# Constant-tile matmuls in TensorE's pauses, and skip and output projection moved behind the last sums, in a four-block convolution and scan kernel

## The chip, the cores and the metric

The kernel runs on one core of a Trainium2 chip. The metric is the device time of one execution in microseconds (us); every comparison is of medians. "PE" is TensorE, "DVE" VectorE, "ACT" ScalarE, "POOL" GpSimd, "SP" the engine that issues most DMAs.

## What is computed

The input is `x`, 8 images of 32 x 32 pixels with 64 channels, float32. Four blocks follow one another, each added to its input after a group normalisation over 32 groups:

```python
x = x + _L0_conv_ref(_gn(x), ...)   # two depthwise 3x3 convolutions, Sobel, 5 diffusion steps
x = x + _L1_conv_ref(_gn(x), ...)   # dense 3x3 convolution, 64 to 64 channels
x = x + _L2_conv_ref(_gn(x), ...)   # layer norm, Mamba block, skip, layer norm, projection
x = x + _L3_conv_ref(_gn(x))        # orthonormal 2-D DCT of each image
```

In the third block a selective scan runs over 1024 positions, for 128 inner channels and 16 states; its output is gated with silu(z), multiplied by the output projection, the scaled normalised input is added (the skip), and after another layer norm the last projection follows:

```python
y = selective_scan(xs, delta, A, Bm, Cm, D) * silu(z)
y = y @ out_proj_w.T + skip_scale * x_norm
y = layer_norm(y, ln_g, ln_b) @ proj_w.T + proj_b
```

## The kernel before, in words

Two images lie side by side on the 128 partitions (64 channels each); such a pair is called `k`, and two pairs make a half `h`. The program treats half 0 and half 1 one after the other. Each engine has its program written out by hand in the order in which it is to run; semaphores join them. `SCANS = 64` scan steps belong to a half: 4 images (`j`) times 16 states.

**The stage in front of the scan** (PE lines 677 to 700). PE ends the dense convolution of pair 1 (`conv_part(1, 1)`, L444), turns the normalised pixels into channels (`xn_channels`, eight 128 x 128 transposes by L433), runs a tiny group mean (L438), the input projection (`in_proj`, L513 for x and L519 for z), the transposes of `n2_pixels(h, 1)` (L433 again), and `x_proj` (L450). DVE follows with `causal` (L1454, then three of L1457) and then the second pair's layer norm; ACT computes silu and the copies (nearly every ACT instruction is recorded at L789).

**The scan** (PE lines 711 to 773). For step s ACT makes the decay, PE brings the row of B into PSUM (`b_rows`, L534, with the constant bf16 tile `sel` of 96 partitions as its weights) or transposes an input scaled by ACT (`turn_scaled`, L433); DVE multiplies where needed (L1493) and scans (L1498); POOL multiplies the states with the row of C (L332) into one of two buffers `HC`, so product s waits for `sum_of(s - 2)`; PE adds the product to PSUM tile `PS[3]` (`sum_of`, L564, four matmuls of 512 columns). The rows of C come by DMA from DRAM, queued by SP. PE calls `fill(s + 2)` and then `sum_of(s - 1)` in loop step s. After 16 steps DVE gates the sum of one image (`gate`, L1502).

At loop step 60 PE also runs `skip(1)` (L572, 16 short matmuls) and `out_proj(h, 2)` (L578, 16 matmuls of 64 columns), between `sum_of(59)` and `fill(63)`; `out_proj(h, 3)` comes after the last sum and needs the last gate.

**Between the halves** DVE goes from the last scan of half 0 to the Sobel sums of half 1 (`sobel_sums`, L224 and L225, then L1338), to the gate (L1502), three more Sobel operations (L1342, L1343, L1345) and the mean of the layer norm (`center`, L1305).

**The last stage** (PE lines 775 to 783) treats pair 1 of half 1 alone: `out_proj(3)`; `center` on DVE (L1305, L1312) with a small ACT step between; a square on ACT; a reduction on DVE (L1317); the variance on ACT, which raises the semaphore `lvar`; the root on POOL (L315); `normalize` on DVE (L1325); `xn2_channels` on PE (L433); a scaling on ACT; `last_proj` (L450); `add_block` on DVE (L1506); `x3_pixels` (L433) and the group statistics; `first_dct` (L600), `keep_x3` (L613), `scale` on ACT, `a2_pixels` (L433), a copy, `second_dct` (L618), two copies and the stores. `center` raises the semaphore `xc`.

Of the kernel before, what the change touches and what calls it, by code (L numbers as in the profile page):

```python
# [15 lines left out]
P = 128  # L16
BLK = L // P
HB = 16
BANK = 512
# [23 lines left out]
def fused_blocks(nc, x, vec, mats, conv_w, in_w, xbc_w, xdt_w, dtp_w, out_w, proj_w, out):  # L43
# [9 lines left out]
    with ctx:  # L53
# [5 lines left out]
        def S(name):  # L59
            if name not in sems:  # L60
                sems[name] = ctx.enter_context(nc.semaphore("s_" + name))
            return sems[name]
# [19 lines left out]
        sel = ctx.enter_context(nc.sbuf_tensor("sel", [96, D_STATE * P], bf16))  # L82

        def mt(name):
            return mat[:, M[name] * P:(M[name] + 1) * P]
# [6 lines left out]
        PS = [ctx.enter_context(nc.psum_tensor(f"ps{i}", [P, 2 * BANK], fp32)) for i in range(4)]  # L92
# [50 lines left out]
        def img(t):  # L143
            return t[:, 0:L].rearrange("p (h w) -> p h w", h=H)
# [7 lines left out]
        def blk(t, k):  # L152
            return t[:, k * P:(k + 1) * P]

        def half(t, n):
            return t[:, n * BANK:(n + 1) * BANK]
# [265 lines left out]
        def _(pe):  # L422
            mm = nc.tensor.matmul
# [16 lines left out]
            def conv_taps(ps, taps, frame, n, chosen, first=0):  # L440

                for tap in chosen:
                    dy, dx = tap // 3, tap % 3
                    last = mm(half(ps, n), taps(tap), frame[:, dy + HB * n:dy + HB * n + HB, dx:dx + W],  # L444
                              start=(tap == first), stop=(tap == 8))
                return last
# [13 lines left out]
            def depthwise(h, k, w, n):  # L460
# [9 lines left out]
                if n == 1:  # L470
                    last.then_inc(S(f"a_conv{w}"), 1)

            def divergence(h, k):
                a = A[k]
                pe.wait_ge(S(f"a{k}_gg1"), 2 * h + 2)
                g, ps = img(a["g"]), img(PS[2 * k])
                for n in range(2):
                    r = slice(HB * n, HB * n + HB)
                    mm(ps[:, r, :], mt("roll_diff"), img(a["g1"])[:, r, :], start=True, stop=False)
                    mm(ps[:, r, 0:31], ident, g[:, r, 1:32], start=False, stop=False)  # L480
                    mm(ps[:, r, 31:32], ident, g[:, r, 0:1], start=False, stop=False)
                    mm(ps[:, r, 1:32], mt("neg_ident"), g[:, r, 0:31], start=False, stop=False)
                    last = mm(ps[:, r, 0:1], mt("neg_ident"), g[:, r, 31:32], start=False, stop=True)
                last.then_inc(S("a_div"), 1)
# [11 lines left out]
            def conv_part(k, n, chosen):  # L496
                return conv_taps(PS[2 * k], lambda tap: blk(convw, tap), frm(D[k]["cfz"]), n, chosen)

            def n2_pixels(h, k):
                pe.wait_ge(S("n2"), 2 * h + k + 1)  # L500
                transposes(D[k]["N2"], PS[2 * k]).then_inc(S("n2T"), 1)
# [20 lines left out]
            def x_proj(h, k, b):  # L522
                i = 2 * h + b
                xs = D[k]["XS"][:, b * L:b * L + L]
                pe.wait_ge(S(f"xs{k}"), i + 1)
                project(PS[2 * k], dtw[:, :], xs).then_inc(S(f"dt{k}"), 1)
                pe.wait_ge(S(f"sz{k}"), i + 1)
                project(PS[2 * k + 1], xbcw[:, :], xs).then_inc(S(f"bc{k}"), 1)
# [28 lines left out]
            def sum_of(h, s):  # L557
                j, first = s // D_STATE, s % D_STATE == 0
                if first:
                    pe.wait_ge(S("y_read"), ONE + 4 * h + j)  # L560
                    plain(pe)
                pe.wait_ge(S("hc"), SCANS * h + s + 1)
                for n in range(2):
                    last = mm(half(PS[3], n), ident, half(HC[s % 2], n), start=first, stop=True, skip_group_check=True)  # L564
                last.then_inc(S("sum"), 1)
                if first:
                    for n in range(2):
                        mm(half(PS[3], n), diagD[:, :], half(two_images(j, "XS"), n), start=False, stop=True, skip_group_check=True)

            def skip(k):  # L570
                for n in range(BLK):
                    mm(blk(PS[2], n), blk(D[k]["XNC"], n), skipI[:, :], start=(n % 4 == 0), stop=False, skip_group_check=True)  # L572

            def out_proj(h, j):
                k, b = j // 2, j % 2
                pe.wait_ge(S("y_read"), ONE + 4 * h + j + 1)
                for n in range(BLK):
                    last = mm(blk(PS[2], n)[:, C * b:C * b + C], blk(D[k]["SZ"], BLK * b + n), outw[:, :],  # L578
                              start=False, stop=True, skip_group_check=True)
                if b == 1:  # L580
                    last.then_inc(S("mo"), 1)

            def xn2_channels(h, k):
                pe.wait_ge(S("xn2"), 2 * h + k + 1)
                transposes(F[k]["XN"], final_ps(h, k)).then_inc(S("xn2T"), 1)
# [39 lines left out]
            for h in range(HALVES):  # L625
# [58 lines left out]
                conv_part(1, 0, range(5, 9))  # L684
                n2_pixels(h, 0)
                conv_part(1, 1, range(9)).then_inc(S("c_conv"), 1)

                xn_channels(h, 0)
                group_mean(D[1], h, 2, 1)
                in_proj(h, 0, 0)  # L690
                n2_pixels(h, 1)
                x_proj(h, 0, 0)
                in_proj(h, 0, 1)
                xn_channels(h, 1)
# [16 lines left out]
                for s in range(1, SCANS):  # L711
                    if s == 2 * D_STATE - 2:
                        pe.wait_ge(S("bcs1"), ONE + 4 * h + 4)
                        plain(pe)
                    fill(h, s + 2)
                    sum_of(h, s - 1)
                    if s == 2:
                        pe.wait_ge(S("rx1"), 2 * h + 2)
                        turn_du(h, 0)
                    if s == 3:  # L720
                        turn_rows(h)
                    if s == 5:
                        pe.wait_ge(S("kept"), 5 * h + ROWS_TURNED)
                        turn_du(h, 1)
                    if s == 23:
                        if h + 1 < HALVES:
                            pe.wait_ge(S("group1"), g_var(h + 1, 0))
                        else:
                            pe.wait_ge(S("kept"), turned(h, 1))
                        turn_du(h, 2)  # L730
                    if s == 28:
                        pe.wait_ge(S("kept"), turned(h, 2))
                        turn_du(h, 3)
                    if s == 32:
                        pe.wait_ge(S("kept"), turned(h, 3))
                        skip(0)
                    if h + 1 < HALVES:
                        if s == 7:
                            pe.wait_ge(S("kept"), turned(h, 1))
                            x_channels(h + 1, 0, PS[2])  # L740
                        if s == 12:
                            group_mean(A[0], h + 1, 0, 0)
                        if s == 15:
                            pe.wait_ge(S("a_x"), 2 * h + 3)
                            pe.wait_ge(S("group0"), g_var(h + 1, 0))
                            x_channels(h + 1, 1, PS[2])
                        if s == 20:
                            group_mean(A[1], h + 1, 0, 1)
                    if s == 33:
                        out_proj(h, 0)  # L750
                    if s == 34:
                        out_proj(h, 1)
                    if s == 41:
                        xn2_channels(h, 0)
                    if s == 44:
                        last_proj(h, 0)
                    if s == 48:
                        group_mean(D[0], h, 3, 0)
                    if s == 50:
                        x3_pixels(h, 0)  # L760
                    if s == 52:
                        first_dct(h, 0)
                    if s == 54:
                        a2_pixels(h, 0)
                    if s == 57:
                        keep_x3(h, 0)
                        second_dct(h, 0)
                    if s == 60:
                        pe.wait_ge(S("ot"), 2 * h + 1)
                        skip(1)  # L770
                        out_proj(h, 2)
                sum_of(h, SCANS - 1)
                out_proj(h, 3)

            h = HALVES - 1
            xn2_channels(h, 1)
            last_proj(h, 1)
            x3_pixels(h, 1)
# [941 lines left out]
```

## Time and profile before

| | |
|---|---|
| runs | 1035.80, 1036.42, 1038.41 us; median 1036.42 |
| the profiled execution | 1035.26 us, its span on the core 1033.2 us |
| mean granted TensorE clock | 0.926 of full speed |
| busy share | PE 82%, DVE 82%, POOL 57%, ACT 55% |
| chain that ended last | PE 42%, DVE 38%, ACT 7%, issue 6%, POOL 6% |
| DMA | 72 GB/s over the span |

The chain says which engine the end waited for at each moment. Granted clock 1.00 is 2.4 GHz and 0.50 is 1.2 GHz; the profile has no other level, and a value between is a stretch that holds both. In the timeline, the bracket behind a row is the idle time in front of it on its engine and what ended it.

### The profile page before, as it was taken

To read this page: it belongs to the slowest core of one execution; us is meant where nothing else is said; L and a number is where in the kernel's file an instruction comes from. 1 tells how busy PE (TensorE), PEld (TensorE's weight loads), DVE (VectorE), ACT (ScalarE), POOL (GpSimd) and SP (SyncE) were. 2 spreads that over 40 slices of the span, in tenths; PEclk is the share of its full clock that TensorE was granted. 3 is DMA by queue.
4 is the path that set the end of the run, shared out by engine and by line. 5 is a ranking of instruction groups with operands and counts; after the bars stand their busy time and mean duration, and the time that the engine had idled before them with its cause. 6 is when DMAs were issued, how large, how long until landed. Compare 5 with 4: busy or idle time off the path is not lost.

```text
span 1033.2 us, 8216 instructions
## 1 busy us (share of the span) xinstructions
PE 843.9 (82%) x2690; PEld 421.4 (41%) x2690; DVE 848.9 (82%) x657; ACT 569.7 (55%) x953; POOL 590.7 (57%) x262
## 2 busy tenths in 40 slices
PE   3986998977288898899889599897738889889955
PEld 2432443433144445446445244343314334545633
DVE  5999887268999898998997978636899999899841
ACT  3733332146748886688575332303684878668802
POOL 2444996020668686877354789501065979677730
PEclk8996999989689999999999899998967999999977
DMA  3000000002344454445100100000113545444411
GB/s 100 1 0 0 0 0 1 0 0 56 79 129 163 139 186 144 144 161 143 44 0 1 20 0 0 0 1 0 56 46 102 176 151 183 143 143 162 146 39 20
DMA packets 33206, 74.35 MB, mean 72 GB/s; under 512 B 15753, under 2 KB 15889, under 8 KB 33169
## 3 DMA queue, kind: packets, MB, share of 16 engines
q1 hardware_dynamic: 31760, 72.58, 21.7%
q0 software_dynamic: 320, 1.05, 0.4%
q8 instruction: 19, 0.31, 0.1%
q10 hardware_dynamic: 1088, 0.26, 0.1%
q14 instruction: 19, 0.15, 0.0%
HBM read 70.73 MB, written 3.15 MB: 72 GB/s over the span
## 4 chain that ended last, share of the span: by engine, by line
PE 42%; DVE 38%; ACT 7%; issue 6%; POOL 6%; DMA 0%; DVEq 0%; SPq 0%; POOLq 0%; ACTq 0%
DVE arena L1498 11%; PE ps L672 9%; PE ps L444 9%; PE ps L564 8%; ACT arena L789 5%; DVE ps L1493 4%; PE ps L433 3%; PE ps L666 3%; POOL arena L332 3%; DVE arena L1457 3%; PE ps L450 2%; DVE arena L1355 2%; POOL dr L315 1%; PE ps L534 1%; DVE arena L1487 1%
## 5 line engine op out<-in xcount | busy, mean ns | idle before, releaser
L332 POOL TENSOR_TENSOR arena<-arena 128x1024 f32<-128x1024 f32 x128 | 304.2, 2383 | 113.9 <-DVE arena L1498 60.7
L1498 DVE TENSOR_TENSOR_SCAN arena<-arena,ps 128x1024 f32<-128x1024 f32 x128 | 289.6, 2281 | 18.0 <-POOL arena L332 8.2
L564 PE MATMUL ps<-arena,mat 128*128 128x512 f32 x512 | 251.7, 616 | 8.8 <-POOL arena L332 7.9
L789 ACT ACTIVATE arena<-arena 128x128 f32<-128x128 f32 (+4 forms) x346 | 146.4, 493 | 106.2 <-DVE arena L1425 75.7
L789 ACT ACTIVATE arena<-arena,Amat 128x1024 f32<-128x1024 f32 x128 | 146.1, 1144 | 88.7 <-DVE arena L1498 85.1
L564 PEld LDWEIGHTS ps<-arena,mat 128*128 128x128 f32 x512 | 95.7, 197 | 90.8 <-issue 68.5
L672 PE MATMUL ps<-arena,mat 128*128 128x512 f32 x240 | 106.3, 592 | 0.0
L1493 DVE TENSOR_TENSOR ps<-arena,ps 128x1024 f32<-128x1024 f32 x72 | 87.2, 1210 | 7.7 <-PE ps L534 5.7
L789 ACT ACTIVATE arena<-ps 128x1024 f32<-128x1024 f32 (+2 forms) x58 | 53.7, 934 | 67.3 <-PE ps L433 22.0
L444 PE MATMUL ps<-arena,diag 128*128 128x512 f32 x192 | 86.6, 609 | 2.1 <-ACT arena L789 2.1
L534 PE MATMUL ps<-arena,sel 96*128 96x512 bf16 x144 | 45.5, 401 | 49.5 <-DVE arena L1498 49.5
L433 PE MATMUL ps<-mat,arena 128*128 128x128 f32 x448 | 61.0, 282 | 26.2 <-DVE arena L1325 14.7
L433 PEld LDWEIGHTS ps<-mat,arena 128*128 128x128 f32 x448 | 52.8, 146 | 53.0 <-issue 29.0
L444 PE MATMUL ps<-arena,convw 128*128 128x512 f32 x144 | 66.9, 621 | 7.2 <-ACT arena L789 7.2
L672 PEld LDWEIGHTS ps<-arena,mat 128*128 128x128 f32 x240 | 45.6, 190 | 57.4 <-issue 57.4
L789 ACT ACTIVATE ROWS<-arena 128x128 f32<-128x128 f32 x224 | 68.2, 389 | 0.0
L444 PEld LDWEIGHTS ps<-arena,diag 128*128 128x128 f32 x192 | 37.0, 195 | 47.6 <-issue 45.4
L321 POOL TENSOR_TENSOR arena<-arena 128x1024 f32<-128x1024 f32 x8 | 21.6, 2704 | 60.0 <-DVE arena L1482 60.0
L315 POOL TENSOR_TENSOR dr<-dv,cpow 128x16 f32<-128x16 f32 x8 | 24.0, 3006 | 55.8 <-DVE dv L1320 43.3
L311 POOL TENSOR_TENSOR dgn<-dgn,cpow 128x1 f32<-128x1 f32 x12 | 7.3, 608 | 85.1 <-DVE dgn L1279 82.5
L348 POOL TENSOR_TENSOR arena<-arena 128x1024 f32<-128x1024 f32 x8 | 25.9, 3242 | 46.4 <-DVE arena L1380 33.0
L534 PEld LDWEIGHTS ps<-arena,sel 96*128 96x128 bf16 x144 | 11.3, 100 | 91.7 <-DVE arena L1498 73.6
(169 smaller groups left out, 1351.2 us busy)
## 6 DMA issues: line engine op xcount, KB each, us to landing
arena<-bc_rows SPq DMA_DIRECT2D x128, 512.0 KB, 3.8
out<-arena SPq DMA_DIRECT2D x28, 64.0 KB, 2.2
xres<-x POOLq DMA_DIRECT2D x4, 256.0 KB, 5.1
bc_rows<-ROWS SPq DMA_DIRECT2D x8, 128.0 KB, 1.9
xres<-x SPq DMA_DIRECT2D x4, 256.0 KB, 4.3
convw<-conv_w SPq DMA_DIRECT2D x1, 576.0 KB
mat<-mats SPq DMA_DIRECT2D x1, 448.0 KB, 3.5
inw<-in_w SPq DMA_DIRECT2D x1, 256.0 KB
```

What stands on the lines that cost most here:

```text
L315: tt(t["r"][:, :], t["v"][:, :], cpow[:, :], ALU.pow).then_inc(S("lrstd"), 1)
L332: tt(HC[s % 2], HS[s % 2], CB[s % 4], ALU.mult).then_inc(S("hc"), 1)
L433: last = nc.tensor.transpose(blk(dst, n), blk(src, n), ident)
L444: last = mm(half(ps, n), taps(tap), frame[:, dy + HB * n:dy + HB * n + HB, dx:dx + W], start=(tap == first), stop=(tap == 8))
L534: last = mm(half(PS[s % 2], n), blk(sel, s % D_STATE), half(two_images(s // D_STATE, "BCS"), n)[0:96, :], start=True, stop=True)
L564: last = mm(half(PS[3], n), ident, half(HC[s % 2], n), start=first, stop=True, skip_group_check=True)
L666: last = mm(half(mix, n), ident, half(a["g"], n), start=False, stop=False, skip_group_check=True)
L672: last = mm(half(mix, n), mt(mname), half(a[src], n), start=False, stop=(name == "e"), skip_group_check=True)
L789: return nc.scalar.activation(out_, in_, func, bias=bias, scale=scale, accum_out=accum_out)
L1457: stt(d["XI"][:, t:L], PS[2 * k][:, 0:L - t], w[3 - t], d["XI"][:, t:L], ALU.mult, ALU.add)\
L1493: tt(PS[q][:, :], two_images(j, "DU"), PS[q][:, :], ALU.mult).then_inc(S("dbu"), 1)
L1498: nc.vector.tensor_tensor_scan(HS[q], DA[q], PS[q][:, :], 0.0, ALU.mult, ALU.add).then_inc(S("scan"), 1)
```

## The change

A new helper `spin(ps, n)` multiplies the first 128 columns of `sel` as weights with 512 columns of `sel`, n times, into the second bank of a PSUM tile, which nobody reads before it is overwritten. It is called at two places in the stage in front of the scan (in both halves) and at three in the last stage, twice behind an added wait. `skip(1)` and `out_proj(h, 2)` leave loop step 60: the first now stands in front of `sum_of(63)`, the second behind it, in both halves.

```diff
+            def spin(ps, n):
+                for _ in range(n):
+                    mm(half(ps, 1), sel[:, 0:P], sel[:, 0:BANK], start=True, stop=True, skip_group_check=True)
...
                 conv_part(1, 1, range(9)).then_inc(S("c_conv"), 1)
+                spin(PS[1], 8)

                 xn_channels(h, 0)
                 group_mean(D[1], h, 2, 1)
                 in_proj(h, 0, 0)
                 n2_pixels(h, 1)
+                spin(PS[3], 14)
                 x_proj(h, 0, 0)
...
-                    if s == 60:
-                        pe.wait_ge(S("ot"), 2 * h + 1)
-                        skip(1)
-                        out_proj(h, 2)
+                pe.wait_ge(S("ot"), 2 * h + 1)
+                skip(1)
                 sum_of(h, SCANS - 1)
+                out_proj(h, 2)
                 out_proj(h, 3)

             h = HALVES - 1
+            spin(PS[0], 10)
+            pe.wait_ge(S("xc"), 4 * h + 4)
+            spin(PS[0], 6)
+            pe.wait_ge(S("lvar"), 4 * h + 4)
+            spin(PS[0], 13)
             xn2_channels(h, 1)
```

## Rows read from the trace of the kernel before

**Rows 1.** The page: granted TensorE clock in tenths, 40 slices of the span.
```profile
PEclk8996999989689999999999899998967999999977
```
**Rows 2.** Windows: us, busy of PE, PEld, DVE, ACT, POOL, then PEclk, DMA share, GB/s.
```profile
211.30:213.60 2.30, 0.00 (x0) 0.00 (x0) 2.30 (x3) 0.00 (x0) 0.42 (x1) 1.00 0.00 0
215.10:221.70 6.60, 6.19 (x9) 3.00 (x10) 2.65 (x7) 3.47 (x3) 0.55 (x1) 0.50 0.00 0
223.50:226.30 2.80, 0.00 (x0) 0.00 (x0) 2.75 (x3) 1.27 (x2) 0.00 (x0) 1.00 0.00 0
...
219.90:262.60 42.70, 27.72 (x72) 11.61 (x71) 38.20 (x35) 27.25 (x27) 3.40 (x2) 0.98 0.12 34
```
**Rows 3.** Timeline, PE, in front of half 0's scan.
```profile
216.10 3.78 PE L513 MATMUL ps<-arena,inw 128*128 128x512 f32 x4
...
226.39 1.98 PE L450 MATMUL ps<-arena,dtw 128*128 128x512 f32 x4 [2.92 <-ACT arena L789]
```
**Rows 4.** Timeline, PE, the input projection in half 1.
```profile
708.19 3.78 PE L513 MATMUL ps<-arena,inw 128*128 128x512 f32 x4 [0.26 <-ACT arena L789]
```
**Rows 5.** Chain: the tile `sel` as weights, at full and at half clock.
```profile
973.42 0.43 PE ps L534 x2
...
785.83 1.03 PE ps L534 x2
```
**Rows 6.** Timeline, last scan steps of half 1.
```profile
980.00 1.08 SPq L259 DMA_DIRECT2D arena<-bc_rows  x2
980.15 1.95 PE L572 MATMUL ps<-skipI,arena 128*128 128x128 f32 x16
...
984.75 2.29 DVE L1498 TENSOR_TENSOR_SCAN arena<-arena,ps 128x1024 f32<-128x1024 f32 x1 [0.79 <-PE ps L433]
...
986.61 4.64 POOL L332 TENSOR_TENSOR arena<-arena 128x1024 f32<-128x1024 f32 x2 [3.60 <-PE ps L564]
...
993.33 1.22 DVE L1502 TENSOR_TENSOR arena<-ps,arena 128x1024 f32<-128x1024 f32 x1 [6.29 <-PE ps L564]
...
994.61 2.00 PE L578 MATMUL ps<-outw,arena 128*128 128x64 f32 x16 [1.32 <-DVE arena L1502]
```
**Rows 7.** Windows, columns as in rows 2: just behind the last C rows.
```profile
985.20:986.40 1.20, 1.20 (x4) 0.51 (x3) 1.20 (x1) 0.00 (x0) 0.00 (x0) 1.00 0.01 3
```
**Rows 8.** Timeline, POOL and DVE, from half 0's last scan to half 1.
```profile
496.51 5.70 POOL L332 TENSOR_TENSOR arena<-arena 128x1024 f32<-128x1024 f32 x2 [3.60 <-PE ps L564]
496.86 3.15 DVE L224 TENSOR_TENSOR arena<-arena 128x1088 f32<-128x1088 f32 x1
...
499.94 3.42 DVE L225 TENSOR_TENSOR arena<-arena 128x1088 f32<-128x1088 f32 x1
```
**Rows 9.** Timeline, DVE, the first of these operations in half 0, POOL idle.
```profile
24.70 1.29 DVE L224 TENSOR_TENSOR arena<-arena 128x1088 f32<-128x1088 f32 x1 [3.72 <-ACT arena L789]
```
**Rows 10.** Windows of the last stage, columns as in rows 2.
```profile
993.30:996.50 3.20, 1.90 (x16) 1.86 (x16) 1.22 (x1) 0.00 (x0) 0.00 (x0) 1.00 0.00 0
996.70:1006.20 9.50, 0.00 (x0) 0.00 (x0) 4.78 (x4) 1.55 (x3) 2.90 (x1) 0.50 0.00 0
...
1013.70:1017.00 3.30, 1.09 (x8) 0.86 (x8) 3.20 (x5) 0.47 (x1) 0.00 (x0) 1.00 0.00 0
```
**Rows 11.** Timeline of the last stage.
```profile
998.15 1.23 DVE L1312 TENSOR_TENSOR ps<-ps,dm 128x1024 f32<-128x1024 f32 x1 [0.28 <-ACT dm L789]
...
1002.11 2.90 POOL L315 TENSOR_TENSOR dr<-dv,cpow 128x16 f32<-128x16 f32 x1 [10.86 <-ACT dv L789]
...
1006.32 1.97 PE L433 MATMUL ps<-mat,arena 128*128 128x128 f32 x8 [9.72 <-DVE arena L1325]
...
1009.59 3.78 PE L450 MATMUL ps<-arena,projw 128*128 128x512 f32 x4 [1.30 <-ACT arena L789]
...
1017.67 3.37 PE L600 MATMUL ps<-mat,arena 128*128 128x128 f32 x16
...
1020.88 1.95 PE L613 MATMUL ps<-mat,arena 128*128 128x128 f32 x16
```

## Prediction

> **What bounds the kernel now.** I read the page first: PE and DVE share the chain (42% and 38%), and the granted clock is full nearly everywhere but in a few slices [rows 1]. Three places matter for this change, so I cut them out with windows and timelines.
>
> In front of the scan PE ends the convolution near 211.2, pauses 2.5 us, runs eight transposes, and from 215.1 to 221.7 the clock is 0.50 [rows 2]. The input projection takes 3.78 us there, where four matmuls of the same shape take 1.98 us at full clock a little later [rows 3]; half 1 shows 3.78 us again [rows 4]. DVE waits for that projection and is then busy for 38.2 of 42.7 us up to the scan [rows 2], so what PE loses, the scan's start loses. A pause alone does not lower the clock: PE was idle from 223.5 to 226.3 at 1.00 [rows 2].
>
> At the end of each half PE runs skip (1.95 us with its latency) and out_proj(2) (as long as out_proj(3), 2.00 us; 3.5 us for both, back to back) in front of the transposes and sums that the last scan and the last products wait for: DVE idles 0.79 us before the last scan and POOL 3.60 us before its last two products [rows 6], half 0 the same [rows 8].
>
> In the last stage everything is one chain. The clock is 0.50 from 996.7 on, while PE has nothing to do, and back at 1.00 in the window from 1013.7 [rows 10]. Three PE steps of the chain run at the lower clock [rows 11]: the transposes (1.97 us, against 1.09 in that later window), the projection (3.78), and, after one more fall, the first DCT (3.37 us for 16 matmuls, where the 16 of L613 take 1.95 right behind).
>
> **The change, part by part.** *Price of a spin.* Two `sel` matmuls of 512 columns take 0.43 us, so one is 0.215 us; the pair costs 1.03 us at half clock with its latency, so some 0.43 us each [rows 5]. 8, 14, 10, 6 and 13 of them are 1.7, 3.0, 2.1, 1.3 and 2.8 us at full clock.
>
> *Spins in front of the scan.* Eight fill 211.0 to 212.8; the transposes come at 213.7, so they cost nothing; if that cover were gone they cost up to 1.7 us. If the clock then holds, the projection ends 1.8 us earlier (3.78 - 1.98) [rows 3]. ACT's silu is not in the way, since DVE's four causal operations (5.2 us) lie between. Today PE waits 2.92 us before `x_proj` [rows 3]. Both the wait's start and its end move forward (by 2.3 and 1.8 us, since L519 is faster too), so fourteen spins run from 221 until 224 and `x_proj` becomes ready at 226.4 - 1.8 = 224.6. They cost nothing too. Bounds of the gain: 0 (clock falls as before) to 1.8 per half. I take 1.8, since the pause of 2.8 us with a full clock [rows 2] shows that some work around a pause is enough, and the spins put work where there was none: 3.6 us for two halves.
>
> *Skip and out_proj(2) out of loop step 60.* The transposes for step 63 no longer stand behind 3.5 us of PE work, so the last scan starts when the one before it ends: 984.0, not 984.75. Sum 60 ends near 983.4, so product 62 starts at 984.0, not 986.6, and product 63 ends at 984.0 + 4.64 = 988.7, not 991.3 [rows 6]. The last two C rows are queued at 980.0, and the DMA engines are idle from 985.2 on [rows 6, 7], so both are there before product 63 begins (986.3). The first of them is needed at 984.0; no row shows its landing, and I count it as just in time. Then PE: sum 62 until 988.1, skip 1.78 until 989.9, sum 63 until 991.6, result at 991.9 where it was 993.3. Here skip stands in front of the last sum and takes back 1.2 us of the 2.6. out_proj(2) runs until 993.4 beside the gate (1.22 us, until 993.15), and out_proj(3) takes its 2.0 us behind both: 995.3, not 996.6 [rows 6]. Gain in half 1: 1.3 us. Bounds: -2.0 (the products don't move: skip costs 1.78 less PE's short wait there, and out_proj(2) outlasts the gate by 0.5) to 1.5. The added wait for `ot` holds nothing up: SP's stores waited for the same copy and are issued before the C rows at 980.0 [rows 6]. SP's, ACT's and POOL's queues are not changed.
>
> *The same at the end of half 0.* Here DVE doesn't wait for the gate but goes on with the Sobel sums, and these collide with POOL: 3.15 and 3.42 us beside POOL's products [rows 8], 1.29 us alone [rows 9]. That is 4.0 us for two products. With product 62 moved beside the scan (which POOL does not slow: 2.29 us, and 4.64 us for two products [rows 6]) only one product collides: DVE would go 496.2, + 1.2 + 1.2 + one product of 2.35, so 501.0 where it was 503.4. Gain 2.3 us (0.8 from the scan, 1.55 from the collision). Sum 63 is ready at 501.9 and the gate comes at 502.2. Bounds: 0.8 (both still collide) to 2.8.
> Each of the two DVE operations is longer by about one POOL product (1.9 and 2.1 us against 2.3), so one product less beside them is about 1.55 to 2 us less.
>
> *Spins in the last stage.* All of DVE's and ACT's steps come 1.3 us earlier: `xc` at 999.4 - 1.3 = 998.1, `lvar` at 1002.1 - 1.3 = 1000.8, `xn2_channels` ready at 1006.3 - 1.3 = 1005.0 [rows 11]. Ten spins follow out_proj(3) until 997.2, six run until 999.4, thirteen until 1003.6. Behind each added wait nothing is queued but the spins and `xn2_channels`, which waits for later work anyway; cover left is 1.4 us. If the clock holds until the projection, transposes save 1.97 - 1.09 = 0.9 and projection 3.78 - 1.98 = 1.8 [rows 3, 10, 11]. No spin stands between the projection and the first DCT; there PE has 1.09 us of work in over 4 us, and that is the window behind which the clock fell before [rows 10]. I therefore leave the first DCT at 3.37 us; if it held, 1.4 us more, as L613's 1.95 us for 16 such matmuls shows [rows 11]. Term: 2.7, bounds 0 to 4.1.
>
> *Sum:* 3.6 + 1.3 + 2.3 + 2.7 = 9.9 us from the profiled execution's 1035.26 us (span 1033.2, 2.1 us around it unchanged): 1025.4. The median of the runs stands 1.2 us above that execution, which would make 1026.5. I take 1025.8, between the two, since one execution doesn't tell which of them is the odd one.
>
> **The rivals.** *Part of the clock gain is lost, and not the same part in each run.* The clock fell behind the pause at 211.3, but not behind the one at 223.5 [rows 2], so where it falls doesn't follow from the pause alone, and eight transposes between two waits stay bare in each spun stretch. One half lost is 1025.8 + 1.8 = 1027.6, the tail lost 1028.5. For it too: the fall at 996.6 came with 1.9 us of PE work in the 3.2 us before [rows 10].
> The Trainium skill (TensorE: Matmul & The Clock Gate, "What's actually happening") says that the activity monitor is free-running and not tied to the kernel's start, so that a change of clock lands at another matmul from run to run. By that rule the median over runs loses one or two microseconds of the clock's 6.3, and runs of the changed kernel differ by that much; no run here shows it yet.
>
> *The spins don't hold the clock at all* (bf16, 96 of 128 rows, no result used: perhaps they don't count). Then only the order pays: 1035.3 - 3.6 = 1031.7, 1032.8 against the median. For it: no row shows such matmuls alone at full clock. Against: in the scan, where they alternate with the sums, the page reads 9 in nearly every slice [rows 1].
>
> *The order gives nothing* (product 62 still waits for its C row, or skip in front of sum 63 takes back all): clock alone, 9.9 - 3.6 = 6.3: 1028.9 to 1030. For it: the DMA engines are still at work until 985 [rows 7].
>
> *Slower than before:* the spins themselves run at half clock and delay the work behind them. Place: the fourteen in front of `x_proj`. At 0.43 us each they take 6.0 us; from 223.4 they end at 229.4 where `x_proj` ran at 226.4: 3.0 us lost in each half [rows 3], and thirteen from 1002.1 end at 1007.7 where the transposes ran at 1006.3, 1.4 us late [rows 11]. With the order's 3.6 us back: 6.0 + 1.4 - 3.6 = 3.8, so 1039.1. It decides where the clock is still 0.50 when the fourteen start; before, it was back at 1.00 behind 221.7, before that point, and PE's 6.2 busy microseconds brought it there [rows 2].
>
> *The change does nothing:* spins not holding the clock and products not moving together: 1035 to 1036.
>
> **How the numbers follow.** Forecast, 1023.3 (first DCT and the order's upper bounds too) to 1027.4: 0.44. Part of the clock gain lost, 1027.4 to 1029: 0.20. Order gives nothing, 1028.9 to 1030.5: 0.12. Spins don't hold, 1031.5 to 1032.8: 0.14. Nothing: 0.06. Slower: 0.04. Range 1022.8 to 1031.8: it takes in the first three cases, and of the fourth its near edge. About 0.3% (3.1 us) is what a measurement of this kernel can tell from no change; all but the last two cases lie beyond it (below 1033.3): faster 0.90, same 0.06, slower 0.04.
>
> **What the profile would show.** The stretch from the convolution's end to `x_proj` at 1.00 in both halves, the first L513 at 1.98 us and DVE's work behind it 1.8 us earlier, counted from the convolution's end; the last scan following the one before without 0.79 us; POOL's last products starting at that scan's start; L224 or L225 at 1.3 us at the half's boundary; L433 at 1.09 and L450 at 1.98 us in the last stage, L600 still 3.37. The forecast is wrong if a window with spins reads 0.50, if PE's idle time before `x_proj` or `xn2_channels` is gone (spins in the way), or if POOL's product 62 waits for a DMA.

## The result, and the profile after

The changed kernel takes 1026.99 us (median of 4 runs, 1025.57 to 1029.02); the kernel before takes 1036.11 us (4 runs, 1035.52 to 1038.41). The ratio is 0.990, 95% interval 0.9884 to 0.9917: faster by 1.0%. The forecast was 1025.8 us, between 1022.8 and 1031.8. The profiled execution took 1025.8 us with a span of 1023.6 us; before it was 1035.26 and 1033.2, so 9.5 us are to be accounted for. The mean granted clock rose from 0.926 to 0.953.

The timeline of the changed kernel in front of half 0's scan (start, length, engine, line; 12 lines of code more shift DVE's and ACT's line numbers, and PE's from L477 on by 6, so L513 is now L519):

```profile
209.78 1.89 PE L477 MATMUL ps<-sel 96*128 96x512 bf16 x8
...
214.84 1.98 PE L519 MATMUL ps<-arena,inw 128*128 128x512 f32 x4 [0.31 <-ACT arena L801]
...
216.86 1.28 DVE L1466 TENSOR_SCALAR arena<-ps,vecs 128x1024 f32<-128x1024 f32 x1 [0.88 <-PE ps L519]
...
219.25 3.19 PE L477 MATMUL ps<-sel 96*128 96x512 bf16 x14
...
223.33 1.98 PE L450 MATMUL ps<-arena,dtw 128*128 128x512 f32 x4 [0.90 <-ACT arena L801]
```

The projection takes 1.98 us where it took 3.78 [rows 3], and both trains of spins end before the work behind them is ready: PE still idles 0.90 us in front of `x_proj` (2.92 before [rows 3]).

The end of half 0 and the start of half 1, where the rows before are [rows 8]:

```profile
488.27 4.47 DVE L1510 TENSOR_TENSOR_SCAN arena<-arena,ps 128x1024 f32<-128x1024 f32 x2
...
491.29 5.71 POOL L332 TENSOR_TENSOR arena<-arena 128x1024 f32<-128x1024 f32 x2 [1.67 <-DMA arena<-bc_rows]
...
492.65 2.13 DVE L224 TENSOR_TENSOR arena<-arena 128x1088 f32<-128x1088 f32 x1
...
494.70 3.44 DVE L225 TENSOR_TENSOR arena<-arena 128x1088 f32<-128x1088 f32 x1
```

The last two scans follow each other without a gap. But POOL's idle time of 1.67 us in front of product 62 now ends with a DMA, the row of C. The first of the two scans, whose states the product needs, ended at 490.6 (488.27 + 2.29), so the row costs the last 0.7 us of that wait, and a part of product 62 still collides with L224 (2.13 us, 3.15 before).

The end of half 1 and the last stage, against [rows 6, 11]:

```profile
972.65 1.08 SPq L259 DMA_DIRECT2D arena<-bc_rows  x2
...
974.33 4.47 DVE L1510 TENSOR_TENSOR_SCAN arena<-arena,ps 128x1024 f32<-128x1024 f32 x2
...
977.25 4.65 POOL L332 TENSOR_TENSOR arena<-arena 128x1024 f32<-128x1024 f32 x2 [1.58 <-DMA arena<-bc_rows]
...
981.47 1.95 PE L578 MATMUL ps<-skipI,arena 128*128 128x128 f32 x16
983.25 1.88 PE L570 MATMUL ps<-arena,mat 128*128 128x512 f32 x4
984.97 3.68 PE L584 MATMUL ps<-outw,arena 128*128 128x64 f32 x32
985.17 1.22 DVE L1514 TENSOR_TENSOR arena<-ps,arena 128x1024 f32<-128x1024 f32 x1 [6.37 <-PE ps L570]
...
998.37 1.09 PE L433 MATMUL ps<-mat,arena 128*128 128x128 f32 x8 [1.26 <-DVE arena L1337]
...
1000.76 1.98 PE L450 MATMUL ps<-arena,projw 128*128 128x512 f32 x4 [1.29 <-ACT arena L801]
...
1004.78 1.81 PE L433 MATMUL ps<-mat,arena 128*128 128x128 f32 x8 [2.04 <-DVE arena L1518]
...
1007.71 3.78 PE L606 MATMUL ps<-mat,arena 128*128 128x128 f32 x16 [0.52 <-ACT arena L801]
```

Here too the first of the two scans ends at 976.6 and the product starts at 977.25, 4.6 us after SP issued the row; the page of the kernel before has a median of 3.8 us from issue to landing for these loads.

The same in windows of the changed kernel (columns as in rows 2):

```profile
988.50:1004.70 16.20, 9.84 (x43) 4.09 (x42) 6.82 (x5) 2.75 (x4) 2.90 (x1) 1.00 0.00 1
1005.00:1011.50 6.50, 5.98 (x28) 5.49 (x27) 2.16 (x8) 1.02 (x1) 0.56 (x1) 0.50 0.00 0
```

Transposes (1.09 us) and projection (1.98) run at the full clock, as far as the spins reach. Then the clock falls at 1005, and now the transposes of `x3_pixels` (1.81 us, 1.09 before) and the first DCT (3.78 us, 3.37 before) run at 0.50. That the spins bring this about isn't shown: kernels without a spin in the last stage show it too (below, the order alone).

**Where the 9.5 us come from.** Each row goes from the end of the row above to the point that it names, in one timeline; the gain is before minus after:

| stretch | before | after | gain |
|---|---|---|---|
| start to the end of half 0's convolution (first L1441, now L1453) | 211.25 | 209.98 | 1.3 |
| to DVE's first causal step, half 0 | 8.67 | 6.88 | 1.8 |
| to the end of half 0's last scan | 277.0 | 275.9 | 1.1 |
| to the end of half 1's convolution | 206.2 | 205.2 | 1.0 |
| to DVE's first causal step, half 1 | 8.82 | 6.88 | 1.9 |
| to the end of half 1's last scan | 275.0 | 274.0 | 1.0 |
| to the last gate | 6.29 | 6.37 | -0.1 |
| to `add_block` | 20.08 | 17.61 | 2.5 |
| to the last copy | 14.06 | 15.17 | -1.1 |

The first row lies in front of everything that the change touches. All fourteen profiles of this case share the code up to there, and in them that point lies between 209.98 and 211.80 us.

### The profile page after: what moved, and what is told of

Read it like the earlier page. It is cut to its first block, busy times and chain, and to the rows that moved or that the text cites. A ratio compares the mean times of both kernels' runs of the same rounds, so it can differ in the third digit from the quotient of the medians.

```text
span 1023.6 us, 8362 instructions
## 1 busy us (share of the span) xinstructions
PE 845.6 (83%) x2763; PEld 423.3 (41%) x2763; DVE 847.7 (83%) x657; ACT 569.6 (56%) x953; POOL 590.9 (58%) x262
## 3 DMA queue, kind: packets, MB, share of 16 engines
HBM read 70.73 MB, written 3.15 MB: 72 GB/s over the span
## 4 chain that ended last, share of the span: by engine, by line
DVE 39%; PE 39%; ACT 7%; POOL 6%; issue 6%; DMA 1%; SPq 1%; DVEq 0%; POOLq 0%; ACTq 0%
DVE arena L1510 12%; PE ps L678 10%; PE ps L444 9%; PE ps L570 6%; ACT arena L801 6%; DVE ps L1505 4%; POOL arena L332 3%; PE ps L672 3%; DVE arena L1469 3%; PE ps L433 3%; DVE arena L1367 2%; PE ps L450 2%; POOL dr L315 1%; DVE arena L1499 1%; DVE arena L1466 1%
```

## The experiments

Eleven variants ran, and the changed kernel once more. The kernel before had medians of 1037.55, 1036.71 and 1037.62 us in the three groups in which they were measured, so ratios are the better measure; a difference between two variants in microseconds is of their medians, and where the ratios say something else, it is told. The theory: spins hold the clock and pay only through the PE steps behind them; the new order pays by the last scan of each half and by the collision of POOL and DVE; the two don't depend on each other. The rivals: one of the two does nothing; or the falls of the clock are accidents of single executions.

**The order alone.**

```diff
-                spin(PS[1], 8)
-                spin(PS[3], 14)
-            spin(PS[0], 10)
-            pe.wait_ge(S("xc"), 4 * h + 4)
-            spin(PS[0], 6)
-            pe.wait_ge(S("lvar"), 4 * h + 4)
-            spin(PS[0], 13)
```

> The change without its five spins and their waits; skip and out_proj(2) stand where the change puts them. Theory (both parts pay, independently): the last scan of each half starts 0.79 us earlier, the boundary between the halves gives 1.0 us more, the last stage gives 0.3 back: 2.3 us below the kernel before; the clock is 0.50 in front of both scans and behind the last gate, as before. Rival (the order alone gives nothing, its gain in the changed kernel was the clock's): within 0.5 us of before.

Measured: 1034.88 us, ratio 0.9977 (0.9964 to 0.9989), 2.4 us (1.1 to 3.7). Its windows show the half clock back in all three places, the last one without the recovery that the kernel before had at 1013.7:

```profile
213.50:220.20 6.70, 5.99 (x10) 2.67 (x9) 2.63 (x8) 3.73 (x3) 0.55 (x1) 0.50 0.00 0
705.10:711.70 6.60, 5.89 (x9) 2.68 (x9) 2.54 (x8) 3.73 (x3) 0.55 (x1) 0.50 0.00 0
995.20:1018.90 23.70, 10.88 (x35) 7.54 (x36) 8.38 (x13) 3.77 (x5) 3.46 (x2) 0.50 0.00 0
```

The order pays as expected, and without any spin. Two more readings of this kernel, in PE's timeline of the last stage:

```profile
1013.09 1.97 PE L433 MATMUL ps<-mat,arena 128*128 128x128 f32 x8 [2.04 <-DVE arena L1511]
...
1016.17 3.38 PE L606 MATMUL ps<-mat,arena 128*128 128x128 f32 x16 [0.68 <-ACT arena L794]
```

The transposes of `x3_pixels` run at half clock here as in the changed kernel, and the first DCT takes as long as before or longer (3.78 us in the kernel with only the front spins), with no spin in the stage. From `add_block` to the last copy it is 14.90 us, and 15.31 and 14.78 in the other two kernels below that have no spin in this stage; the kernel before, at 14.06, is the lowest of the four.

**The spins alone**, with skip and out_proj(2) back in loop step 60.

```diff
+                    if s == 60:
+                        pe.wait_ge(S("ot"), 2 * h + 1)
+                        skip(1)
+                        out_proj(h, 2)
                 sum_of(h, SCANS - 1)
-                out_proj(h, 2)
                 out_proj(h, 3)
```

> The five spins with skip and out_proj(2) back in loop step 60. Theory: 1.8 and 1.9 us in front of the two scans, 2.7 us in the last stage, less up to 1.0 us where the first DCT runs wholly at half clock: 5.4 to 6.4 us below before. Rival (without the new order out_proj(3) alone stands before the ten spins, the clock has fallen there already, and they run at 0.50): only the 3.7 us of the front stages, and the ten spins take 4.3 us.

Measured: 1033.91 us, ratio 0.9961 (0.9946 to 0.9976), 4.0 us: less than the theory's 5.4. The nine runs fall into two groups, four from 1031.26 to 1031.76 and five from 1033.91 to 1034.78. The profile is of the second group, and shows three losses. The boundary of the halves, from half 0's last scan to half 1's convolution, took 207.70 us, 206.24 before. In half 0 the clock fell in spite of the eight spins (8.4 us to the first causal step, 6.9 in half 1). And in the last stage:

```profile
1001.09 5.73 PE L477 MATMUL ps<-sel 96*128 96x512 bf16 x13 [1.18 <-ACT dv L802]
1006.61 1.60 PE L433 MATMUL ps<-mat,arena 128*128 128x128 f32 x8
```

```profile
996.50:1000.80 4.30, 2.73 (x12) 0.90 (x10) 2.82 (x3) 1.32 (x3) 0.00 (x0) 1.00 0.00 0
1000.90:1007.60 6.70, 6.51 (x18) 3.03 (x19) 1.23 (x1) 0.13 (x1) 2.90 (x1) 0.50 0.00 0
```

The clock fell in the pause of 1.18 us behind the six spins, the thirteen took 5.73 us instead of 2.98, and the transposes started with no idle time in front of them, 1.3 us after DVE's `normalize` (1004.04 + 1.23) had made them ready. That is the mechanism of my slow rival, in one place and for 1.3 us. The ten spins took 2.32 us, so they did not start at half clock, as the rival had it. The first group of runs would be the executions without some of these losses; their mean granted clock is 0.947 to 0.948 against 0.936 to 0.942 in the second, which fits, but they have no profile.

**Only the spins in front of the scan** (the edit above, and):

```diff
-            spin(PS[0], 10)
...
-            spin(PS[0], 13)
```

> Only the eight and the fourteen spins in front of the scan, in both halves. Theory: 3.7 us below before, the first L513-type projection at 1.98 us in both halves. Rival (the fall moves elsewhere): the projection is fast but the clock falls somewhere later before the scan, and less than 2 us are left.

Measured: 1033.76 us, ratio 0.9971 (0.9960 to 0.9982), 3.0 us. Both halves show 6.88 us to the first causal step, so the 3.7 us are there in the stage; in the boundary of the halves 1.5 us went the other way (207.75 us from scan end to convolution's end, 206.24 before, with one more stretch at 0.50 at 524 to 527). The spins alone gave hardly more than the spins in front of the scan: by the ratios, the last stage's were worth 1 us with the old order, by the medians nothing (1033.91 and 1033.76 us), and the intervals overlap.

**The whole change without the spins of the last stage.**

```diff
                 out_proj(h, 3)

             h = HALVES - 1
-            spin(PS[0], 10)
...
-            spin(PS[0], 13)
             xn2_channels(h, 1)
```

> The whole change without the spins and waits of the last stage. Theory (the spins there give 2.7 us with the new order, less 1.0 us at the first DCT): 1.5 to 2.5 us above the changed kernel (1027.0 to 1027.3); xn2's transposes 1.97 and the last projection 3.78 us. Rival (behind the new order out_proj(2) and out_proj(3) alone keep the clock up): within 0.5 us of the changed kernel.

Measured: 1029.54 us, ratio 0.9927 (0.9912 to 0.9942), against 0.9900 and 0.9906 for the change itself: they are worth 2.2 to 2.8 us. Gate to `add_block` is 20.13 us again, 17.6 in the changed kernel. This stretch shows the effect of the spins most steadily: 20.08 to 20.28 us in the four profiled kernels without spins there, 17.61 or 17.62 in nine of the ten profiles with them, and 19.20 in the kernel with spins alone. This profile shows a front stage that was lost with the spins in it, as the one with spins alone:

```profile
216.60:219.80 3.20, 3.15 (x4) 1.51 (x5) 0.51 (x3) 1.95 (x3) 0.55 (x1) 0.50 0.00 0
```

**The changed kernel again**, with no edit.

> The changed kernel again, unaltered, as the neighbour of the next three and for the spread of its executions. Theory (the clock's falls lie at points that are not tied to the program, and the spun stretches are too thin to be safe in each run): executions spread over 3 to 5 us, in steps of about 1.5 to 2 us, and this profile shows the clock falling at other points than the first one. Rival (the program sets the falls): the same falls as in the first profile, spread under 1 us.

Measured: 1027.25 us (6 runs, 1026.31 to 1028.79), ratio 0.9906 (0.9891 to 0.9921). With the first measurement ten executions lie between 1025.57 and 1029.02, 3.5 us; the steps that I had expected in them don't stand out. The same program, the same stretch of the diffusion steps, first and second profile:

```profile
80.00:86.70 6.70, 3.78 (x4) 1.17 (x4) 6.70 (x7) 1.24 (x1) 0.17 (x1) 0.50 0.00 0
87.00:90.00 3.00, 0.20 (x1) 0.24 (x2) 2.93 (x4) 1.45 (x2) 2.74 (x2) 1.00 0.00 0
```

```profile
79.00:95.40 16.40, 9.30 (x11) 3.62 (x12) 16.34 (x13) 7.61 (x11) 8.51 (x3) 0.50 0.00 0
```

Near the same work the clock was at 1.00 in one execution and at 0.50 in the other, and half 0's convolution ended at 209.98 and at 211.4. So some falls move from run to run, and the 1.3 us in the first row of the table are not the change's. Most falls do not move: between the two scans the clock is at 0.50 from 581.7 to 592.0 us in the first profile and from 583.7 to 594.0 in the second, where the same work comes 1.6 to 1.9 us later, and the stretch behind `add_block` starts 2.2 and 2.3 us behind that step. So of the theory and the rival each has a part.

**More spins in front of the scan** (11 for 8, 4 behind `xn_channels`, 17 for 14).

```diff
-                spin(PS[1], 8)
+                spin(PS[1], 11)
                 xn_channels(h, 0)
+                spin(PS[3], 4)
...
-                spin(PS[3], 14)
+                spin(PS[3], 17)
```

> The whole change with more spins in front of the scan: 11 for 8, 4 new ones behind xn_channels, 17 for 14, sized so that they end before the work behind them is ready. Theory (thin stretches let the clock fall in some runs): both front stages take 6.9 us from the convolution's end to DVE's first causal operation in every profile; the median is 0.5 to 1.5 us below the changed kernel's, with less spread. Rival (the eight were enough, or spins have no such effect): no difference.

Measured: 1026.57 us (5 runs, 1026.10 to 1027.25), ratio 0.9900 (0.9884 to 0.9915). The median is 0.7 us under its neighbour's and the spread 1.2 us against 2.5, as expected but inside the intervals. The profiles say more. Ten profiles here, the changed kernel's two among them, have the eight spins; in their twenty stages the clock fell in three, all of them in half 0 (8.4 to 8.5 us to the first causal step instead of 6.9). The two kernels with the dense spins show 6.9 in four of four. Four of four is no proof at a loss of three in twenty.

**More spins in the last stage.**

```diff
-            spin(PS[0], 10)
+            spin(PS[0], 13)
...
-            spin(PS[0], 6)
+            spin(PS[0], 11)
...
-            spin(PS[0], 13)
+            spin(PS[0], 18)
             xn2_channels(h, 1)
+            spin(PS[1], 6)
             last_proj(h, 1)
+            spin(PS[1], 9)
             x3_pixels(h, 1)
+            spin(PS[1], 3)
             group_mean(D[1], h, 3, 1)
+            spin(PS[1], 3)
             first_dct(h, 1)
```

> The whole change with more spins in the last stage: 13, 11 and 18 for 10, 6 and 13, and 6, 9, 3 and 3 new ones behind the second transposes, the last projection, x3_pixels and the group mean. Theory: the clock stays at 1.00 from the last gate to the second DCT; transposes 1.09, first DCT 1.95 instead of 3.4 to 3.8 us: 2.5 us below the changed kernel. Rival (the new spins delay the steps they stand before): PE's idle time before L433 or L600 is zero and the gain is under 1 us or a loss.

Measured: 1023.98 us (5 runs), ratio 0.9881 (0.9865 to 0.9898), 3.3 us below its neighbour (2.6 by the ratios).

```profile
988.78 9.71 PE L477 MATMUL ps<-sel 96*128 96x512 bf16 x42
998.66 1.09 PE L433 MATMUL ps<-mat,arena 128*128 128x128 f32 x8 [0.18 <-DVE arena L1341]
...
1005.11 1.09 PE L433 MATMUL ps<-mat,arena 128*128 128x128 f32 x8
...
1007.82 1.95 PE L606 MATMUL ps<-mat,arena 128*128 128x128 f32 x16
```

Both steps that ran at half clock in the changed kernel are at full clock; `add_block` to the last copy takes 13.13 us, against 15.17 and 15.03 in the changed kernel's two profiles and 14.06 before. So 1.9 to 2.0 of the 3.3 us are shown in the stage. Which of the seven trains of spins are needed for it was not tried.

**Twice the spins in front of x_proj.**

```diff
-                spin(PS[3], 14)
+                spin(PS[3], 28)
```

> The whole change with 28 spins for 14 in front of x_proj. The profile leaves PE 0.90 us idle there; 14 more cost 3.0 us at full clock. Theory (spins are hidden only as long as the pause lasts, then PE's time is paid in full): x_proj starts 2.1 us later in each half; the chain runs through DVE beside it, so between 2 and 4.2 us above the changed kernel. Rival (PE is not bound there, DVE's work hides it): under 1 us.

Measured: 1028.32 us, ratio 0.9919 (0.9902 to 0.9937), 1.1 us above its neighbour, less than I expected. `x_proj` starts 2.0 us later, 15.3 us behind the convolution's end instead of 13.4, with no idle time in front of it, and the first scan comes 57.91 us behind the first causal step instead of 57.03: 0.9 us per half are paid, DVE's other work hides the rest.

```profile
225.31 1.88 PE L450 MATMUL ps<-arena,dtw 128*128 128x512 f32 x4
```

Neither side is right: the price of an uncovered spin is paid in full by PE and by less than half by the kernel.

**Without the fourteen.**

```diff
-                spin(PS[3], 14)
```

> The whole change without the fourteen spins in front of x_proj. PE then idles some 4 us there, in both halves. Theory: the clock falls there, x_proj (eight matmuls, 3.9 us at full clock) runs partly at 0.50 while DVE does the second pair's layer norm; part is hidden, so 0.5 to 2 us above the changed kernel. Rival (the eight are enough, or DVE hides it all): within 0.4 us.

Measured: 1027.96 us, ratio 0.9912 (0.9897 to 0.9926), 0.7 us above the changed kernel (0.6 to 1.2 by the ratios), with intervals that overlap.

```profile
224.65 3.61 PE L450 MATMUL ps<-arena,dtw 128*128 128x512 f32 x4 [3.92 <-ACT arena L800]
```

```profile
221.00:224.80 3.80, 0.15 (x1) 0.15 (x2) 3.70 (x5) 1.15 (x1) 0.00 (x0) 1.00 0.00 0
225.00:228.20 3.20, 3.20 (x5) 1.15 (x4) 2.11 (x2) 1.02 (x1) 0.00 (x0) 0.50 0.00 0
713.10:716.30 3.20, 3.20 (x4) 1.25 (x5) 2.11 (x2) 1.02 (x1) 0.00 (x0) 0.50 0.00 0
```

A faster projection makes the pause behind it longer (3.92 us; 2.92 before [rows 3]), and now the clock falls there, in both halves. The fourteen spins pay only because the eight have done their work; 57.7 us from the first causal step to the first scan instead of 57.0 is what they save.

**The stores behind the last rows of C.**

```diff
                 for s in range(4, SCANS):
                     c_row(h, s)
-                    if s == SCANS - 3:
-                        store_out(h, 0)
+                store_out(h, 0)
```

> The whole change, and SP queues the eight stores of pair 0 behind the last two rows of C instead of in front of them. Theory (POOL's product 62 waits for its C row, which stands behind the stores): product 62 starts when its scan ends, 0.7 us earlier, and at the half's boundary DVE's L224 and L225 collide with one product only: 1.4 us below the changed kernel, no DMA named as releaser of L332 there. Rival (the rows are slow by themselves, or the stores then delay something in the next half): no gain, or up to 1 us lost.

Measured: 1027.54 us (5 runs), ratio 0.9904 (0.9886 to 0.9923): no gain in the time. But POOL's wait is no longer for a DMA (its line is now L331, DVE's scan L1509):

```profile
979.45 4.66 POOL L331 TENSOR_TENSOR arena<-arena 128x1024 f32<-128x1024 f32 x2 [1.04 <-DVE arena L1509]
```

At the boundary of the halves the same holds, and L224 is nearly free of the collision:

```profile
495.67 1.49 DVE L224 TENSOR_TENSOR arena<-arena 128x1088 f32<-128x1088 f32 x1
...
497.08 3.45 DVE L225 TENSOR_TENSOR arena<-arena 128x1088 f32<-128x1088 f32 x1
```

From the last scan's end to the gate it is 5.83 us, 6.37 in the changed kernel; the boundary of the halves took 204.95 us, 205.20 there. Some 0.8 us are there in the stages, and its profile lost a front stage (8.45 us). 0.8 us could not be told from none by these runs.

**And skip in front of sum 62.**

```diff
                     fill(h, s + 2)
+                    if s == SCANS - 1:
+                        pe.wait_ge(S("ot"), 2 * h + 1)
+                        skip(1)
                     sum_of(h, s - 1)
```

> The late stores and skip(1) in front of sum 62, where PE waits 1.3 to 1.8 us for POOL, instead of between sums 62 and 63. Theory: the last gate ends 1.2 us earlier against the kernel with late stores and 1.7 us against the changed one; at the boundary of the halves DVE doesn't wait for the gate, so nothing there: 2 us below the changed kernel in all. Rival (sum 62 comes later by as much as sum 63 comes earlier): no gain over the late stores.

Measured: 1026.22 us (5 runs, 1024.59 to 1028.52), ratio 0.9897 (0.9883 to 0.9911). In the stage the effect is clear:

```profile
979.96 1.95 PE L577 MATMUL ps<-skipI,arena 128*128 128x128 f32 x16
981.74 3.95 PE L569 MATMUL ps<-arena,mat 128*128 128x512 f32 x8
...
985.73 1.23 DVE L1514 TENSOR_TENSOR arena<-ps,arena 128x1024 f32<-128x1024 f32 x1 [4.63 <-PE ps L569]
```

Last scan to gate is 4.64 us, 6.37 in the changed kernel: 1.7 us, as expected, but the medians give 1 us (0.3 to 0.9 by the ratios) with intervals that overlap.

**All together** (dense spins in both stages, late stores, skip in front of sum 62).

> The dense spins in both stages, the late stores and skip(1) in front of sum 62, together. Theory (the effects add): dense_tail gave 3.3 us, dense_front 0.7, late stores with skip 2: 1021 to 1022, 1.4% below before. Rival (they share one path or the dense spins now meet work that is ready earlier): above 1023.

Measured: 1023.98 us (4 runs, 1023.79 to 1024.27), ratio 0.9873 (0.9859 to 0.9887): 1.3% below the kernel before, the lowest ratio and the smallest spread of all. It is above the 1021 to 1022 that adding would give. Its windows are at full clock through all three stages; the last one reads:

```profile
988.00:1016.00 28.00, 25.91 (x136) 14.20 (x135) 9.29 (x13) 6.92 (x8) 3.46 (x2) 1.00 0.00 1
```

Last scan to gate is 4.64 us and `add_block` to the last copy 13.14. Against the kernel with the dense last stage the ratio is lower by 0.0008 with intervals of 0.0014 to 0.0017 to each side, so that the two differ isn't shown. The gate's 1.7 us are in its profile; at the boundary of the halves it took 205.68 us against 205.23 there, and half 0's convolution ended 0.9 us later, and these are the places that vary from run to run.

## Why the prediction was right, point by point

*Spins in front of the scan, 3.6 us.* The table has 1.8 and 1.9 us. Eight spins end 0.78 us before the transposes, fourteen 0.90 us before `x_proj`, near the cover that the sum had. But it doesn't hold in each execution: in three of twenty stages the clock fell all the same. That is the rival of partial loss. Its premise, that a fall isn't tied to the program, is shown for some falls by two profiles of one program, and most of the others stood still.

*Last scan without its 0.79 us.* Right: the scan stretches are shorter by 1.1 and 1.0 us, of which 0.8 is this; the rest I can't assign.

*The collision with POOL, 1.55 us more.* Measured 1.0. The step that failed is "product 62 starts at 984.0 ... just in time": it starts 0.7 us behind its scan, when its row of C has landed, and that row is queued behind eight stores of pair 0. In the kernel with late stores it starts with its scan's end (979.45), and L224 takes 1.49 us, near the 1.2 of the sum. L225 stays at 3.4 us there too, since product 63 runs beside it, as the sum had it. The prediction names "if POOL's product 62 waits for a DMA" as a sign of being wrong; it came, and for this term the forecast was wrong, by 0.5 us. Spins at 0.50, another such sign, came in the kernel with spins alone, and not in this one.

*The end of half 1, 1.3 us.* Mis-sized: 0.8 from the scan, -0.1 to the gate, and -0.2 behind it, since two out_proj in a row end 3.5 us after the gate's start and one ended 3.3 us after it. The sum had 5.6 us from the last scan's end to the gate, with skip in front of the last sum in it; the changed kernel has 6.37, and the kernel with late stores 5.83, so the row of C is most of the difference. The kernel with skip in front of sum 62 shows that the place between the last two sums cost 1.2 us.

*Spins in the last stage, 2.7 us.* Gate to `add_block` gained 2.5 us, 2.7 if the 0.2 of out_proj is taken off. *The first DCT as before, 0:* wrong by 1.1 us between these two profiles. I left its time at 3.37 us, but it had not been wholly at half clock, and the transposes before it had run at full clock; in the changed kernel nearly all of both is at 0.50. That the change costs this isn't shown: the three other kernels without spins in the last stage take 14.78 to 15.31 us from `add_block` to the last copy, and the changed kernel 15.17 and 15.03. The one profile of the kernel before, 14.06, was a favourable base. The dense kernel shows 1.95 and 1.09 us there.

*The base.* 1.3 us of the profile's 9.5 lie in front of everything changed, so the change itself made 8.2 us between these two profiles, where the sum had 9.9; that the profiled time met the sum is in part this luck. Over all runs the medians differ by 9.1 and 9.5 us in the two measurements (1036.11 - 1026.99, 1036.71 - 1027.25), by the ratios 10.4 and 9.7, so the runs can't tell the sum's 9.9 from what was measured. But three of its terms came out lower in this profile, by 0.5 us (collision), 0.8 (end of half 1) and 1.1 (first DCT), and nothing in the sum makes up for them: that the total fits all the same is in part luck.

*The rivals.* That spins don't hold the clock is out: the changed kernel has 16 us at 1.00 in the last stage, where each of the four profiled kernels without spins reads 0.50 for at least 13.7 us. That the order gives nothing is out: 2.4 us alone. That the two parts don't depend on each other is not borne out, though not excluded either: alone they gave 2.4 us (1.1 to 3.7) and 4.0 us (2.5 to 5.6), together 9.7 to 10.4 by the ratios. The profile of the spins alone has the missing time in three places (half 0's front stage, the last stage, the boundary of the halves), in the first two as falls of the clock; whether the old order brings them, and by what way, stays open. The slow rival's mechanism was seen once, with the old order, for 1.3 us and not for 3.8: in front of the scan, where most of that price lay, the clock was back before the fourteen spins began, in each profile that lost the stage.

## What to carry to other kernels

Filler matmuls on a constant tile pay where a PE step on the path runs at half clock behind a pause: read that step's time at both clocks, and size each train so that it ends just before the awaited work is ready. Look at the pause that a faster step opens behind it: without the fourteen spins it lost 0.7 us per half of what the eight had won. Look too at the steps that no train covers: the kernel with trains there, and with longer ones before them, gained another 1.9 to 2.0 us in that stage. And take more than one profile of the kernel before, since a single one can be a favourable base at one stage. When work is moved off a path, ask what that path waits for next; here it was a DMA behind eight stores in the same queue, and skip in front of the last sum.

## What the runs showed of the hardware that I had not expected

The clock fell behind a pause of only 1.18 us that followed six spins (1.3 us of work), in the kernel with spins alone, while a pause of 2.8 us in front of half 0's `x_proj` left it at 1.00 [rows 2], and the same 1.18 us behind six spins did so in the changed kernel. So the pause alone doesn't tell where the clock falls. A single execution can be 1 to 2 us off its program's median: 26 runs of the kernel before in one group lay between 1033.59 and 1039.13 us. How much of that is the clock isn't shown: the changed kernel's first four runs go with it (0.953 at 1025.57 and 1025.80 us, 0.946 at 1028.17 and 1029.02), but the kernel before reads 0.926 at 1035.41 us and at 1038.30 us.
The Trainium skill (TensorE: Matmul & The Clock Gate, "What's actually happening") has the monitor free-running; the changed kernel's two profiles agree in one place, with 1.00 and 0.50 between 87 and 90 us, while most falls stand at the same work in both.

POOL's product and DVE's operation with two SBUF operands delayed each other by whole instructions: with product 62 moved forward by part of its length, L224 got shorter by 1.0 us (3.15 to 2.13) and L225, beside product 63, stayed at 3.4. POOL pays as well: product 63 takes 3.4 us beside them (5.71 us for the two), 2.35 alone.
The Trainium skill (SBUF — State Buffer, "Who interferes with whom") says that a DVE instruction with two SBUF inputs contends with a GpSimd instruction that reads SBUF, and that the pair of ports which they share is an exclusive lock; these rows agree with it.
